# An adaptive attention layer with a mixture-of-experts FFN: the counts and ranks of twelve batches moved ahead of the last batch's mixes

## The chip, the cores and the metric

The program runs on one core of one Trainium2 chip. The core has a matrix engine (TensorE, PE in the rows), VectorE (DVE), ScalarE (ACT), GpSimd (POOL) and SyncE (SP), each with its own queue of instructions; they meet through semaphores only. The metric is the device time of one execution in microseconds; lower is better. All arithmetic is float32, part of it in the form fp32r that splits a value into a high and a low part.

## The reference

Sixteen batches of 128 rows with 128 features go through two layers with one residual:

```
xn   = layernorm(x)
q    = l2norm(xn @ Wq) * q_scale            (16 heads of 64)
k, v = xn @ Wkv, one null key and value in front; k l2-normed
sim  = 8 * q.k + relative-position bias, causal mask
y    = layernorm(softmax(sim) @ v @ Wout) * g_out
out  = x + shared_expert(y) + sum over the two best of 7 experts: w_e * expert_e(y)
expert(h) = (silu(h @ g.T) * (h @ u.T)) @ d.T          (128 -> 352 -> 128)
w: softmax over the router's logits, the two largest, renormalised
```

Of the 2048 rows each goes to two of seven experts, so which rows an expert works on is known only on the chip.

## The kernel before

**Attention.** Every engine runs `step(t)` for t = 0 to 18 (`run_steps`, L280). Step t makes the queries of batch t, the scores of batch t - 1, the turned and mixed probabilities of batch t - 2 (`turn_p`, `mix`), and the projection of batch t - 3. So steps 16, 17 and 18 only drain. In step 17 TensorE also turns the normalised outputs y of batches 0 to 11 (`turn_y`, L1265) and makes their router logits (`logits`, L1274). Step 18 has for TensorE only `mix(3, 3)` and `project()` of batch 15, for ACT `keep_oT(1, 3)`, for VectorE `choose(0)` (L930: the two best experts of each row of batches 0 to 11) and `keep_y()` (L1021: the last projection out of bank 7).

**Routing.** The batches are in two parts, k = 0 (batches 0 to 11) and k = 1 (12 to 15). For a part: `choose(k)` marks the chosen experts; `count(k)` on TensorE (L1282) multiplies these marks by a triangle of ones and by a full matrix of ones, which gives each row's place among the rows of its expert and the totals; `rank(k)` on VectorE (L954) turns that into the row number where the row is to be sent; `weigh(k)` on ACT (L743) and `share_out(k)` on VectorE (L979) make the two shares; `mark(k)` (L949) writes the row's destination beside it. Before the change `count(0)`, `weigh(0)`, `mark(0)`, `rank(0)` and `share_out(0)` stand after step 18; count(0) and rank(0) use bank 6, into which the mixes also write.

**Sends.** GpSimd then issues 32 indirect DMAs (L530), one for each batch and choice: 12 and 12 of part 0, 4 and 4 of part 1. Each writes 128 rows with 128 features, share and destination into a DRAM buffer sorted by expert. The first of a part waits for `row_index_made` and `send_made`. Before send i it also waits until (i - 8) // 2 shared tiles are kept (`down_kept`, at most 13).

**Tiles.** `run_tiles` (L296) runs 16 shared tiles (one a batch, the shared expert) and then 38 routed tiles of 128 rows. A tile goes through four stages, one step each: the high and low parts of its input (yh on ACT L771, yl on VectorE L1118), gate and up matmuls (12 short groups with the down matmuls, L1181), silu and product, turn, down matmuls and the sum (shared: into xs, L1141). Between the first shared tiles stand the routing of part 1 (`between`: `root_y(1)` and `scale_y(3)` after step 0, `turn_y(3)` after 1, `logits(3)` and `choose(1)` after 2, `count(1)` and `rank(1)` after 3, `list_tiles` after 5). The first routed tile needs all 32 sends landed and the list of tiles; SyncE then loads its rows (L381).

L1181 and L1178 are the helpers `mm` and `turn`, so all matmuls and turns have these lines; the tile names tell them apart.

Of the kernel before, what the change touches and what calls it, by code (L numbers as in the profile page):

```python
# [26 lines left out]
def adaln_ffn_kernel(nc: bass.Bass, x, cond, mask, g_norm, wq, wkv, q_scale, k_scale, null_bias, w0, b0, g0,  # L27
# [47 lines left out]
    with ctx:  # L75
# [211 lines left out]

        def logit_bank(b):
            return 5 if b < Y_FIRST else 6

        def turned_bank(t, c):

# [282 lines left out]
        def _(act):  # L575
# [69 lines left out]
            def keep_yT(g):  # L645
                act.wait_ge(y_turned, g + 1)
                nc.scalar.activation(YT[:, g * 512:(g + 1) * 512], bank[y_bank[g]][:, :], ACT.Copy).then_inc(yT_kept, 1)

            def step(t, p, on):
                q = 1 - p  # L650

                def keep_q(c):
                    if on(0):
                        half = slice(c * HALF * P, (c + 1) * HALF * P)
                        act.wait_ge(q_made, 2 * t + c + 1)
                        need(act, scored, NCH * (t - 2) + 2 * c + 2)
                        nc.scalar.activation(qT[:, p, half].rearrange("p (k s) -> p k s", k=HALF),
                                             bank[4][:, :].rearrange("p (k s) -> p k s", k=HALF)[:, :, ::-1], ACT.Copy).then_inc(q_kept, 1)
# [10 lines left out]
                def exp(c, back):  # L669
                    if on(back):  # L670
                        b = t - back
                        act.wait_ge(maxed, NCH * b + c + 1)
                        for h in range(c * HC, (c + 1) * HC):
                            v = Pb[:, b % 2, h, :]
                            last = nc.scalar.activation(v, v, ACT.Exp, bias=low[:, b % 2, h:h + 1],  # L675
                                                        accum_out=den[:, b % 2, h:h + 1])
                        last.then_inc(exped, 1)
# [26 lines left out]

                if t == NB + 1:
                    exp(3, 2)
                keep_q(0)
                keep_pT(0)
                square_q(0)
# [30 lines left out]

            run_steps(act, step)

            def weigh(k):  # L743
                b = slice(PARTS[k].start, PARTS[k].stop)
                act.wait_ge(gap_made, k + 1)
                nc.scalar.activation(share[:, 1, b], share[:, 3, b], ACT.Exp).then_inc(gap_exped, 1)

            act.wait_ge(biasm_first, 2 * NB)
            act.wait_ge(biasm_made, 2 * NB)
            act.wait_ge(y_normed, Y_FIRST // 4)  # L750
            nc.scalar.activation(send[0][1][:, :, 0:D], y_sb[:, 0:Y_FIRST, :], ACT.Copy).then_inc(send_made[0][1], 1)
            weigh(0)

            def step(u, m, lap, kind):
                if kind(3):
# [36 lines left out]
        def _(dve):  # L792
            done = 0

            def own(ins):

                nonlocal done
                done += 1
                ins.then_inc(dve_step, 1)
                dve.wait_ge(dve_step, done)  # L800
# [129 lines left out]
            def choose(k):  # L930
                b, n = slice(PARTS[k].start, PARTS[k].stop), len(PARTS[k])
                dve.wait_ge(logits_made, k + 1)
                lb, eb = L[:, b, :], equal[:, b, :]
                own(nc.vector.tensor_tensor(lb, bank[logit_bank(b.start)][:, 0:NB * NE].rearrange("p (b e) -> p b e", b=NB)[:, b, :],
                                            rbr[:, :].unsqueeze(1).to_broadcast([P, n, NE]), ALU.add))
                for m in range(TOP):

                    own(nc.vector.tensor_reduce(best[:, m, b], lb, AX_X, ALU.max))
                    own(nc.vector.tensor_tensor(eb, lb, spread(best[:, m, b], NE), ALU.is_equal))
                    own(nc.vector.scalar_tensor_tensor(eb, eb, -float(NE),  # L940
                                                       iota7[:, :].unsqueeze(1).to_broadcast([P, n, NE]), ALU.mult, ALU.add))
                    own(nc.vector.tensor_reduce(share[:, 0, b], eb, AX_X, ALU.min))
                    own(nc.vector.tensor_tensor(chosen[:, m, b, :], eb, spread(share[:, 0, b], NE), ALU.is_equal))
                    if m == 0:
                        own(nc.vector.scalar_tensor_tensor(lb, chosen[:, 0, b, :], 2 * NEG, lb, ALU.mult, ALU.add))
                nc.vector.tensor_tensor(load[:, b, :], chosen[:, 0, b, :], chosen[:, 1, b, :], ALU.add).then_inc(load_made, 1)
                nc.vector.tensor_tensor(share[:, 3, b], best[:, 1, b], best[:, 0, b], ALU.subtract).then_inc(gap_made, 1)

            def mark(k):  # L949
                b = slice(PARTS[k].start, PARTS[k].stop)  # L950
                for m in range(TOP):
                    nc.vector.tensor_copy(send[k][m][:, :, DEST_AT].bitcast(I32), dest[:, m, b]).then_inc(send_made[k][m], 1)

            def rank(k):  # L954
                b, n = slice(PARTS[k].start, PARTS[k].stop), len(PARTS[k])
                up, pad = run_up[k], PADS[k]
                dve.wait_ge(sort_consts, 5)
                dve.wait_ge(ranks_made, k + 1)
                tot = bank[6][:, (2 * k + 1) * P:(2 * k + 1) * P + n * NE].rearrange("p (b e) -> p b e", b=n)
                base = eoff[:, :] if k == 0 else run_up[0][:, 0, PADS[0] + Y_FIRST - 1, :]  # L960
                nc.vector.tensor_copy(totals[:, b, :], tot)
                nc.vector.tensor_tensor(up[:, 0, pad, :], tot[:, 0, :], base, ALU.add)
                own(nc.vector.tensor_copy(up[:, 0, pad + 1:pad + n, :], tot[:, 1:n, :]))
                own(nc.vector.tensor_tensor(place[:, b, :], bank[6][:, 2 * k * P:2 * k * P + n * NE].rearrange("p (b e) -> p b e", b=n),
                                            totals[:, b, :], ALU.subtract))
                side, far = 0, 1
                while far < n:
                    own(nc.vector.tensor_tensor(up[:, 1 - side, pad:pad + n, :], up[:, side, pad:pad + n, :],
                                                up[:, side, pad - far:pad - far + n, :], ALU.add))
                    side, far = 1 - side, 2 * far  # L970
                assert side == 0
                own(nc.vector.tensor_tensor(place[:, b, :], place[:, b, :], up[:, side, pad:pad + n, :], ALU.add))
                for m in range(TOP):
                    last = nc.vector.tensor_tensor(placed[:, m, b, :], chosen[:, m, b, :], place[:, b, :], ALU.mult)
                own(last)
                own(nc.vector.tensor_reduce(row_of[:, :, b], placed[:, :, b, :], AX_X, ALU.add))
                nc.vector.tensor_copy(row_index[:, :, b], row_of[:, :, b]).then_inc(row_index_made, 1)
# [9 lines left out]
            def step(t, p, on):  # L987
# [33 lines left out]
                def keep_y():  # L1021
                    if on(3):
                        dve.wait_ge(y_made, t - 2)
                        nc.vector.tensor_copy(y_sb[:, t - 3, :], bank[7][:, 0:D])
                        nc.vector.bn_stats(y_bst[:, t - 3, :], bank[7][:, 0:D]).then_inc(y_kept, 1)
                        if t > 3 and t - 4 != Y_FIRST - 1:
                            gather_y(t - 4)
# [25 lines left out]
                    nc.vector.tensor_scalar(router_wT[:, 0:NE], bank[2][:, 0:NE], gocol[:, 0:1], None, ALU.mult).then_inc(router_kept, 1)  # L1053
                if t == NB + 2:
                    choose(0)
                keep_y()
                if t > 1:
                    invert(0, 1)
# [42 lines left out]
                nc.vector.tensor_scalar(tile_expert[:, RING:RING + ROUTED], tile_float[:, :], 1.0, None, ALU.add)  # L1101
                nc.vector.scalar_tensor_tensor(tile_row[:, :], iota_tile[:, :], float(P), tile_skip[:, :], ALU.mult, ALU.add).then_inc(table_made, 1)

            mark(0)
            rank(0)
            share_out(0)
            own(nc.vector.memset(h_sb[:, :, I:ICH * IC], 0.0))

            def step(u, m, lap, kind):
# [65 lines left out]
        def _(pe):  # L1175
# [4 lines left out]
            def mm(out, a, b, start, stop):  # L1180
                return nc.tensor.matmul(out, a, b, start=start, stop=stop, skip_group_check=True)  # L1181
# [100 lines left out]
            def count(k):  # L1282
                pe.wait_ge(load_made, k + 1)
                pe.wait_ge(sort_consts, 5)
                b, n = slice(PARTS[k].start, PARTS[k].stop), len(PARTS[k])
                load_flat = load[:, b, :].rearrange("p b e -> p (b e)")
                mm(bank[6][:, 2 * k * P:2 * k * P + n * NE], before[:, :], load_flat, True, True)
                mm(bank[6][:, (2 * k + 1) * P:(2 * k + 1) * P + n * NE], ones[:, :], load_flat, True, True).then_inc(ranks_made, 1)

            def step(t, p, on):  # L1290
                q = 1 - p
# [90 lines left out]
                def turn_sums():  # L1382
                    if on(0):
                        pe.wait_ge(sums_kept, t + 1)
                        turn(bank[7][:, P:2 * P], sums_sb[:, :]).then_inc(sums_turned, 1)

                queries(0)
                turn_p(0)
                mix(3, 3)
# [37 lines left out]


            pe.wait_ge(oT_kept, 2 * NB)
            count(0)  # L1430

            expert_regs = [pe.alloc_register(f"expert_reg{k}") for k in range(RING + 2)]

            def load_experts(r):
# [87 lines left out]
```

## Time and profile before

| | |
|---|---|
| median of 3 runs | 437.17 us (432.62 to 437.86) |
| profiled execution | 437.97 us |
| its span | 436.2 us |
| TensorE busy, matmul / weight load | 359.3 us (82%) / 297.6 us (68%) |
| VectorE busy | 291.2 us (67%) |
| ScalarE busy | 279.5 us (64%) |
| GpSimd busy | 228.7 us (52%) |
| mean granted clock of TensorE | 0.923 |

In the span, attention lasts until about 277 us, the shared tiles until about 321, the routed tiles from 328 to about 420, and the last 16 us collect the results. The busy shares are means over these stages; what matters for a change between attention and tiles is the order of a few dozen instructions there, and so the rows come from timelines.

### The profile page before, as it was taken

Reading aid. Unit: us, or ns where it says so; the run is one execution under the profiler, and the core shown is the slowest. Engines: PE = TensorE matmul, PEld = TensorE weight load, DVE = VectorE, ACT = ScalarE, POOL = GpSimd, SP = SyncE. Lnnn points to the kernel's source line nnn. Section 1 sums busy time; section 2 is a strip of 40 time slices with the busy share of each in tenths; the row PEclk is TensorE's granted clock in tenths of the full one; section 3 lists DMA queues with packets and bytes.
Section 4 is the critical chain, followed back from the end, with each engine's and each line's share of the span. In section 5 each row is a group of like instructions: output and inputs, shape, how many; then the busy total and the mean of one; then the engine's idle time right before and its main releaser. Section 6 shows DMA issues by size and latency. Waiting matters only on the chain. (4 is left out here: it accounts for less than half of the span.)

```text
span 436.2 us, 10247 instructions
## 1 busy us (share of the span) xinstructions
PE 359.3 (82%) x2921; PEld 297.6 (68%) x2922; DVE 291.2 (67%) x1144; ACT 279.5 (64%) x935; POOL 228.7 (52%) x253
## 2 busy tenths in 40 slices
PE   0286776999999999999997989587948999999930
PEld 0275655677777777777775647487948999899920
DVE  2838385888888898888889893568524555555514
ACT  1374684999999999999996783345523444444410
POOL 5024833688766667667772542076750444444430
PEclk9997995999999999999999687859997999999995
DMA  6726199970000000000000000011111222121118
GB/s 187 198 78 198 52 221 207 207 141 2 2 2 2 3 2 2 3 0 2 2 2 2 1 2 0 2 50 51 55 43 45 57 61 61 49 60 58 39 19 271
DMA packets 39479, 26.54 MB, mean 61 GB/s; under 512 B 4465, under 2 KB 37131, under 8 KB 39439
## 3 DMA queue, kind: packets, MB, share of 16 engines
q1 hardware_dynamic: 33680, 19.55, 20.1%
q0 software_dynamic: 2240, 4.23, 2.9%
q10 hardware_dynamic: 3518, 2.26, 1.8%
q8 instruction: 20, 0.33, 0.3%
q14 instruction: 21, 0.16, 0.1%
HBM read 12.89 MB, written 13.54 MB: 61 GB/s over the span
## 5 line engine op out<-in xcount | busy, mean ns | idle before, releaser
L675 ACT ACTIVATE p_space<-p_space,low 128x129 f32<-128x129 f32 x256 | 99.0, 392 | 6.3 <-DVE low L1011 6.3
L494 POOL TENSOR_TENSOR p_space<-p_space,inv 128x516 f32<-128x516 f32 x64 | 67.0, 1049 | 66.1 <-DVE inv L1019 66.1
L1007 DVE SCALAR_TENSOR_TENSOR p_space<-bank,rn,biasm_space 128x129 f32<-128x129 f32 x256 | 72.1, 344 | 22.2 <-PE bank L1181 21.9
L485 POOL TENSOR_TENSOR biasm_space<-bias,madd 128x516 f32<-128x516 f32 x64 | 75.6, 1193 | 7.4 <-DVE p_space L1007 7.3
L536 POOL DMA_INDIRECT result_rows<-oT_space,dest_ring x38 | 37.3, 982 | 60.3 <-DVE dest_ring L1147 60.3
L760 ACT ACTIVATE biasm_space<-bank 128x384 f32<-128x384 f32 x54 | 26.6, 492 | 58.3 <-PE bank L1178 58.2
L1178 PE MATMUL bank<-ident,p_space 128*128 128x128 f32 (+1 forms) x272 | 48.5, 297 | 2.4 <-POOL p_space L494 2.1
L675 ACT ACTIVATION_READ_ACCUMULATOR p_space<-p_space,low 128x1 f32 x256 | 48.6, 190 | 0.0
L1181 PE MATMUL bank<-DT,biasm_space 128*128 (+1 forms) x324 | 46.5, 281 | 1.3 <-ACT biasm_space L760 1.3
L1181 PE MATMUL bank<-GH,yh 128*128 (+1 forms) x108 | 41.3, 382 | 6.8 <-DVE yl L1118 6.8
L690 ACT ACTIVATE pT<-bank 128x512 f32<-128x512 f32 x64 | 37.3, 583 | 13.7 <-PE bank L1181 12.5
L1011 DVE TENSOR_REDUCE low<-p_space 128x4 f32<-128x516 f32 x64 | 44.2, 691 | 2.2
L1181 PEld LDWEIGHTS bank<-DT,biasm_space 128*128 128x128 f32 x324 | 43.6, 196 | 2.3 <-issue 1.8
L1181 PE MATMUL bank<-pT,V 128*64 128x256 f32 x256 | 44.6, 433 | 0.1
L1181 PEld LDWEIGHTS bank<-KB,q_space 64*128 64x128 f32 x512 | 33.5, 193 | 15.8 <-issue 9.8
L1181 PE MATMUL bank<-KB,q_space 64*128 64x129 f32 x512 | 42.8, 298 | 1.1 <-DVE p_space L1007 1.1
L1178 PEld LDWEIGHTS bank<-ident,p_space 128*128 128x128 f32 (+1 forms) x272 | 31.3, 147 | 12.6 <-issue 4.6
L1181 PE MATMUL bank<-xnT,wq_sb 128*128 128x128 f32 x256 | 36.3, 286 | 1.6 <-ACT sq L666 1.6
L1178 PE MATMUL bank<-ident,biasm_space 128*128 128x128 f32 x179 | 31.4, 293 | 6.6 <-DVE biasm_space L884 3.9
L1181 PEld LDWEIGHTS bank<-xnT,wq_sb 128*128 128x128 f32 x256 | 31.9, 196 | 7.2 <-issue 5.2
L1181 PE MATMUL bank<-GH,yl 128*128 (+1 forms) x108 | 36.2, 335 | 0.0
L1181 PE MATMUL bank<-GL,yh 128*128 (+1 forms) x108 | 36.2, 335 | 0.0
(217 smaller groups left out, 682.8 us busy)
## 6 DMA issues: line engine op xcount, KB each, us to landing
sent_rows<-fill_row SPq DMA_DIRECT2D x2, 1950.0 KB, 23.0
sent_rows<-fill_row SPq DMA_DIRECT2D x2, 1885.0 KB, 19.1
q_space<-sent_rows SPq DMA_DIRECT2D x38, 65.0 KB
xs<-in_x_dram SPq DMA_DIRECT2D x4, 256.0 KB, 6.4
bias<-bias_rows SPq DMA_DIRECT2D x1, 1024.0 KB, 6.0
xnT<-result_rows ACTq DMA_DIRECT2D x4, 256.0 KB, 6.1
xn<-result_rows SPq DMA_DIRECT2D x4, 256.0 KB, 5.2
out_dram<-xs SPq DMA_DIRECT2D x4, 256.0 KB, 2.4
```

Of the source, the lines that this page charges most:

```text
L485: nc.gpsimd.tensor_tensor(biasm[:, b % 2, heads, :], bias[:, heads, :], madd[:, b:b + 1, :].to_broadcast([P, HC, KEYS]), ALU.add).then_inc ...
L494: nc.gpsimd.tensor_tensor(v, v, spread(inv[:, b % 2, heads], KEYS), ALU.mult).then_inc(p_normed, 1)
L536: nc.gpsimd.indirect_dma_start(out=result_dram[:, :], out_offset=bass.IndirectOffsetOnAxis(ap=dest_ring[:, m:m + 1], axis=0), in_=result[: ...
L675: last = nc.scalar.activation(v, v, ACT.Exp, bias=low[:, b % 2, h:h + 1], accum_out=den[:, b % 2, h:h + 1])
L690: nc.scalar.activation(pT[:, c % 2, :], bank[turned_bank(t, c)][:, :], ACT.Copy).then_inc(p_kept, 1)
L760: nc.scalar.activation(hT[:, (m - 3) % 2, :], bank[4 + (m - 3) % 2][0:IC, 0:ICH * P], ACT.Copy).then_inc(hT_kept, 1)
L1007: last = nc.vector.scalar_tensor_tensor(Pb[:, q, h, :], src, rn[:, q, h:h + 1], biasm[:, q, h, :], ALU.mult, ALU.add)
L1011: nc.vector.tensor_reduce(low[:, q, c * HC:(c + 1) * HC], Pb[:, q, c * HC:(c + 1) * HC, :], AX_X, ALU.max, negate=True).then_inc(maxed, 1)
L1178: return nc.tensor.transpose(out, in_, ident[0:n, 0:n])
L1181: return nc.tensor.matmul(out, a, b, start=start, stop=stop, skip_group_check=True)
```

## The change

It moves the routing of part 0 into step 18. On TensorE `count(0)` now stands at the head of step 18, ahead of `mix(3, 3)` and `project()` of batch 15. On ACT `weigh(0)` stands at the head of that step. On VectorE `mark(0)`, `rank(0)` and `share_out(0)` follow `choose(0)` directly and so come before `keep_y()` of batch 15. As the mixes still use bank 6 then, the counts of part 0 go into bank 3, and TensorE first waits until ACT has copied the turned y out of it; part 1 keeps bank 6. The conditions before the sends are unchanged.

```diff
+        def count_bank(k):
+            return (3, 6)[k]
...
+            def weigh(k):
+                b = slice(PARTS[k].start, PARTS[k].stop)
+                act.wait_ge(gap_made, k + 1)
+                nc.scalar.activation(share[:, 1, b], share[:, 3, b], ACT.Exp).then_inc(gap_exped, 1)
...
+                if t == NB + 2:
+                    weigh(0)
                 keep_q(0)
                 keep_pT(0)
                 square_q(0)
...
-            weigh(0)
...
-                tot = bank[6][:, (2 * k + 1) * P:(2 * k + 1) * P + n * NE].rearrange("p (b e) -> p b e", b=n)
+                tot = bank[count_bank(k)][:, (2 * k + 1) * P:(2 * k + 1) * P + n * NE].rearrange("p (b e) -> p b e", b=n)
...
                 if t == NB + 2:
                     choose(0)
+                    mark(0)
+                    rank(0)
+                    share_out(0)
                 keep_y()
...
-            mark(0)
-            rank(0)
-            share_out(0)
             own(nc.vector.memset(h_sb[:, :, I:ICH * IC], 0.0))
...
-                mm(bank[6][:, 2 * k * P:2 * k * P + n * NE], before[:, :], load_flat, True, True)
-                mm(bank[6][:, (2 * k + 1) * P:(2 * k + 1) * P + n * NE], ones[:, :], load_flat, True, True).then_inc(ranks_made, 1)
+                if k == 0:
+                    pe.wait_ge(yT_kept, y_bank.index(count_bank(0)) + 1)
+                mm(bank[count_bank(k)][:, 2 * k * P:2 * k * P + n * NE], before[:, :], load_flat, True, True)
+                mm(bank[count_bank(k)][:, (2 * k + 1) * P:(2 * k + 1) * P + n * NE], ones[:, :], load_flat, True, True).then_inc(ranks_made, 1)
...
+                if t == NB + 2:
+                    count(0)
                 queries(0)
                 turn_p(0)
                 mix(3, 3)
...
             pe.wait_ge(oT_kept, 2 * NB)
-            count(0)
```

## Rows read from the trace of the kernel before

**Rows 1.** The page: busy tenths and TensorE's granted clock in 40 slices.
```profile
PE   0286776999999999999997989587948999999930
...
PEclk9997995999999999999999687859997999999995
```
**Rows 2.** Chain of waits, in time: start us, length us, what.
```profile
309.63 1.63 PE bank L1181 x12
...
311.60 1.63 PE bank L1181 x12
...
323.30 2.27 DMA sent_rows<-p_space,row_index
...
326.44 1.86 DMA q_space<-sent_rows
...
328.82 3.04 PE bank L1181 x12
```
**Rows 3.** GpSimd's timeline: start us, length us, engine, what, [idle before <-releaser].
```profile
282.54 1.21 POOL L530 DMA_INDIRECT sent_rows<-bias,row_index  x1 [18.28 <-DVE bias L984]
...
296.69 0.96 POOL L530 DMA_INDIRECT sent_rows<-bias,row_index  x1 [0.30 <-issue]
299.16 0.96 POOL L530 DMA_INDIRECT sent_rows<-madd,row_index  x1 [1.51 <-DVE xs L1141]
...
304.29 0.96 POOL L530 DMA_INDIRECT sent_rows<-madd,row_index  x1 [0.38 <-DVE xs L1141]
...
323.30 0.96 POOL L530 DMA_INDIRECT sent_rows<-p_space,row_index  x1 [0.30 <-issue]
```
**Rows 4.** VectorE's timeline, from the choice of part 0 to shared tile 1.
```profile
271.53 0.16 DVE L947 TENSOR_TENSOR share<-best 128x12 f32<-128x12 f32 x1
277.18 0.29 DVE L1024 COPY xn<-bank 128x128 f32<-128x128 f32 x1 [5.49 <-PE bank L1181]
...
277.68 0.14 DVE L952 COPY bias<-dest 128x12 int32<-128x12 int32 x1
...
277.86 0.24 DVE L961 COPY o_space<-bank 128x84 f32<-128x84 f32 x1
...
281.58 0.11 DVE L1107 MEMSET biasm_space<- 128x64 f32 x1
281.73 0.29 DVE L1118 TENSOR_TENSOR yl<-xnT,yh 128x128 fp32r<-128x128 f32 x1
...
285.56 0.28 DVE L1118 TENSOR_TENSOR yl<-xnT,yh 128x128 fp32r<-128x128 f32 x1
...
298.09 0.28 DVE L1141 TENSOR_TENSOR xs<-bank,xs 128x128 f32<-128x128 f32 x1
```
**Rows 5.** TensorE's timeline, attention's last steps to the first routed tile.
```profile
255.30 0.66 PE L1178 MATMUL bank<-ident,p_space 128*128 128x128 f32 x4 [2.05 <-POOL p_space L494]
...
272.03 1.95 PE L1181 MATMUL bank<-pT,V 128*64 128x256 f32 x8
...
277.07 0.68 PE L1181 MATMUL bank<-o_space 128*128 128x84 f32 x4
282.17 0.63 PE L1181 MATMUL bank<-GH,yh 128*128 128x352 f32 x1 [4.42 <-DVE yl L1118]
...
289.01 1.71 PE L1181 MATMUL bank<-router_wT,xnT 128*128 128x7 f32 x8
...
328.35 0.47 PE L1178 MATMUL bank<-ident,q_space 128*128 128x128 f32 x1 [6.93 <-DMA q_space<-sent_rows]
```
**Rows 6.** ScalarE's timeline in step 18 and after.
```profile
274.03 0.60 ACT L702 ACTIVATE oT_space<-bank 128x512 f32<-128x512 f32 x1 [1.36 <-PE bank L1181]
...
276.00 0.50 ACT L771 ACTIVATE yh<-xnT 128x128 fp32r<-128x128 f32 x2
```
**Rows 7.** Busy us (count) by stretch: PE, PEld, DVE, ACT, POOL; clock; DMA; GB/s.
```profile
257.00:258.00 1.00, 1.00 (x5) 0.24 (x4) 0.97 (x5) 1.00 (x6) 1.00 (x2) 0.50 0.00 0
281.00:294.00 13.00, 10.39 (x41) 9.90 (x42) 8.37 (x44) 5.40 (x11) 8.89 (x9) 0.50 0.12 42
```

More of the change, by code:

```diff
@@ L741, in _ @@
             run_steps(act, step)
[L743 to L746, printed above, removed]
             act.wait_ge(biasm_first, 2 * NB)
@@ L963, in rank @@
                 own(nc.vector.tensor_copy(up[:, 0, pad + 1:pad + n, :], tot[:, 1:n, :]))
-                own(nc.vector.tensor_tensor(place[:, b, :], bank[6][:, 2 * k * P:2 * k * P + n * NE].rearrange("p (b e) -> p b e", b=n),
+                own(nc.vector.tensor_tensor(place[:, b, :], bank[count_bank(k)][:, 2 * k * P:2 * k * P + n * NE].rearrange("p (b e) -> p b e", b=n),
                                             totals[:, b, :], ALU.subtract))
```

## The prediction

> **What bounds the kernel now.** I read the page's slices first. They show two holes of TensorE behind the attention steps, one in slice 26 and one in slice 30 of 40 (272 to 283 and 316 to 327 us), with a low granted clock in the slices around the first [rows 1]. Then I read the chain of waits backwards from the first routed tile. The group of matmuls at 328.82 is released by the load of the tile's rows (1.86 us, issued at 326.44), which waited for the landing (2.27 us) of the last of 32 indirect sends that GpSimd issues [rows 2]. TensorE's turn of that tile starts at 328.35 after 6.93 us of idle, so it had run out of shared tiles at 321.4 [rows 5]. So ahead of 328 us the row of sends decides, not the tiles.
>
> What sets the row of sends is in GpSimd's timeline [rows 3]. Sends go out every 1.265 us: (323.30 - 304.29) / 15 = 1.267. The first starts at 282.54 after 18.28 us of idle, released by the shares that VectorE writes. The twelfth starts at 296.69; the thirteenth, which would follow at 297.95, starts at 299.16, because its pace condition wants two shared tiles kept. The seventeenth waits 0.38 us instead of the usual 0.30, so the fourth tile's condition just touches. From 299.16 the last send is 19 sends later: 299.16 + 19 x 1.267 = 323.2, against 323.30. **Hence the time of the second shared tile, not the start of the sends, sets the first routed tile.**
>
> What sets the second shared tile is in VectorE's timeline [rows 4]: its sum into xs is written at 298.09, at the end of an unbroken line of VectorE work that began when the last projection was ready at 277.18. That line is: keep_y 0.50 us (to 277.68), mark(0) 0.18 (to 277.86), rank(0) and share_out(0) 3.72 (to 281.58), the memset 0.15, and then yl of tile 0 at 281.73, root_y(1) and scale_y(3) until yl of tile 1 at 285.56, and so on. TensorE starts tile 0 at 282.17 after 4.42 us of waiting for that yl [rows 5].
>
> **The change, part by part.** The profiled run took 437.97 us for a span of 436.2, 0.8 above the median of 437.17; I work out a difference in its trace and take it off the median.
>
> (a) choose(0) ends with the gap at 271.53 + 0.16 = 271.7 [rows 4]. VectorE then idles for 5.49 us until the last projection. The change puts mark(0), rank(0) and share_out(0) in this hole.
>
> (b) TensorE's count(0), four matmuls and 0.68 us at the full clock [rows 5], moves ahead of mix(3, 3) of batch 15. TensorE runs eight mix matmuls without a gap from 272.03, the last four of which (273.0 on) belong to this step. It reaches the count at 273.0, when VectorE has finished the choice; bank 3 was copied out in step 17, ahead of the logits. So neither of its waits costs anything. But the count is in line before mix, keep_oT and project. Nothing hides it: it delays y_made by its own length. It runs mostly at 1.2 GHz, where eight logits matmuls of the same weight size take 1.71 us, so four take 0.85 [rows 5]. Ends: 0.5 (three quarters of the 0.68, the first of four weight loads under the mix before) to 0.85; I take 0.7, between them. The 0.68 us that it frees after the projection is worth nothing, since TensorE waits there anyway.
>
> (c) ACT's weigh(0) moves ahead of keep_oT(1, 3). ACT is idle for 1.36 us before that copy (274.03), and the gap is made at 271.7, before this hole opens at 272.7 [rows 6]. It is one activation over 128x12, shorter than the 0.25 us of one yh copy, and lies in the hole: cost 0, and 0.25 without it. The two yh copies at 276.00 move by the 0.7 us and stay ahead of VectorE.
>
> (d) VectorE: the count ends at 273.0 + 0.7 = 273.7, rank(0) starts 0.11 later as it does now (277.75 to 277.86), and rank and share_out take 3.72 as now: until 277.5. The delayed projection comes at 277.18 + 0.7 = 277.88. So the whole 3.9 us fits, with 0.35 us to spare; if the count is slower, both move together.
>
> (e) After the projection: keep_y 0.50, memset 0.15, then yl of tile 0 at 277.88 + 0.65 = 278.53 instead of 281.73. **Shift: 3.9 removed (0.18 + 3.72) less 0.7 added = 3.2 us.** All of TensorE, ACT and VectorE from tile 0 on goes by these, so the second shared tile moves by 3.2.
>
> (f) GpSimd: row_index is ready at about 276.8 and the shares at 277.4, so the first send moves from 282.54 to about 278.4, 4.1 us sooner. Send 13 waits for the second tile as before: 299.16 - 3.2 = 295.96. The additional 0.9 us of head start is lost in a longer wait. The last send: 320.1. GpSimd has nothing else queued behind these sends but the results of routed tiles.
>
> (g) The routed tiles start at 328.35 - 3.2 = 325.15, with shared tiles done at 318.2, so the 6.9 us hole stays. From there on no instruction changes: full carry to the end.
>
> Sum: 437.97 - 3.2 = 434.8 for the profiled execution, 437.17 - 3.2 = **434.0** by the median.
>
> **Where a rule weighs against this sum.** The granted clock is 0.50 (1.2 GHz) in 257 to 258 us, soon after an idle of only 2.05 us on TensorE that ended at 255.30; it is also 0.50 in all of 281 to 294, from within the 4.42 us hole on, and full in the slices behind it [rows 1, 5, 7]. After the change the hole is some 1.1 us (277.8 to 279.0), but yl of tile 1 still comes 3.8 us behind that of tile 0 [rows 4], so TensorE idles again behind one tile's matmuls, and small ones follow. I therefore take the clock to stay at its low level for tiles 0 to 2, as now.
> The Trainium skill ("TensorE: Matmul & The Clock Gate", HAM oscillation) says the opposite may hold: it is long idle gaps between bursts of matmuls that bring the clock to its half level, so a kernel that closes them stays warm. By it tiles 0 to 2 would run at full clock; the trace of before does not bear out that short gaps are harmless.
>
> **The rivals.**
> Rival 1, clock stays at 2.4 GHz. Twelve matmuls of a tile take 3.04 us at the low clock and 1.63 at the full one [rows 2]. On the way to the second tile lie half of such a group (0.7 us saved), the logits of 1.71 us, which in the same ratio save 0.8, and turns that save some 0.3: 1.8 in all. The row of sends itself allows it: first send 278.4 plus 12 x 1.267 plus 0.25 for the longer first one is 293.9 for send 13 instead of 299.16, a limit of 5.3 us. Gain 3.2 + 1.8 = 5.0, time 437.2 - 5.0 = 432.2. For it: the longest hole goes. Against it: the 2.05 us idle above.
>
> Rival 2, part of it is given back: VectorE's line meets a count that comes late (TensorE waits at count(0) for choose(0) when its turns and mixes run at full clock, up to 1 us, which mix and projection behind it then pay), or the tiles after the second pace the sends, since the seventeenth has no slack now. Gain 1.5: 435.7.
>
> Rival 3, no gain: the routed start does not hang on tile 2 but on something unmoved. Against it stand the 6.93 us hole and the arithmetic of 19 sends. Time 437.2.
>
> Rival 4, slower, by the pace condition with the clock low for longer. A tile period at the full clock is 311.60 - 309.63 = 1.97 us [rows 2], less than the 2.53 of two sends; at 1.2 GHz it is 1.97 + 1.41 = 3.38, and then every tile paces the row and adds 0.85. Because the fourth tile has no slack, the change turns to a loss from about four additional slow tiles on (4 x 0.85 = 3.4). Six of them (5.1): 437.2 - 3.2 + 5.1 = 439.1. For it: the tiles start sooner while the clock's rise, between 294 and 295 now, need not. Against: from the fourth tile on TensorE is dense, and the clock is full from there [rows 1].
>
> **How the numbers follow.** Chances: forecast 0.63, rival 1 0.13, rival 2 0.11, rival 3 0.05, rival 4 0.08. The forecast's own width: the count's two ends give 433.8 to 434.2, and the three runs shown lie between 432.62 and 437.86, so a median can be 2 us off: 432 to 436. The range takes in most of rival 1 and rivals 2 and 3, and leaves rival 4 out: 430.8 to 437.4. Two per cent, about what a measurement of this kernel can tell from no change, is 8.7 us. No case reaches 428.4 or 445.9; I leave 0.02 and 0.02 for what I don't see: faster 0.02, same 0.96, slower 0.02.
>
> **What would show it.** Right: VectorE has rank(0) ending before 277.9 with the last projection kept at about 277.9; yl of tile 0 near 278.5; TensorE's wait before tile 0 down from 4.4 to about 1 us; first send near 278.4, a wait of 1.5 to 2 us before the thirteenth, last send near 320; the routed tiles' turn near 325.2 after the same hole of 6.9. Wrong: a wait of TensorE at the count, mixes delayed by more than 0.9, a granted clock that is full in 281 to 291 (rival 1), still half after 298 (rival 4), or a routed start that stays at 328.

## The result and the profile after

The changed kernel takes 433.35 us (median of 20 runs, 429.1 to 435.11) against 437.4 (20 runs, 432.62 to 438.29) before. The ratio on record is 0.9936, 95% interval 0.9913 to 0.996: 1.7 to 3.8 us faster, 2.8 in the middle, where the two medians lie 4.05 us apart. It is clear of no change and below two per cent. Forecast were 434.0 and 3.2 us. The executions of one kernel spread here with the mean granted clock: in 35 further runs of the kernel before, those at 0.923 take about 437.3 us and those at 0.938 about 432. The profiled executions (clock 0.923 before, 0.926 after) differ by more than the ratio says, 431.6 against 436.2 us of span, and the first thing to read is how much of that 4.6 is the change.

VectorE's timeline of the changed kernel, from the choice of part 0 to shared tile 1 (columns as in [rows 4]):

```profile
267.31 0.25 DVE L938 TENSOR_TENSOR o_space<-bank,rbr 128x84 f32<-128x84 f32 x1 [2.88 <-PE bank L1185]
...
270.97 0.17 DVE L956 COPY madd<-dest 128x12 int32<-128x12 int32 x1
273.22 0.24 DVE L965 COPY o_space<-bank 128x84 f32<-128x84 f32 x1 [2.08 <-PE bank L1185]
...
276.82 0.17 DVE L989 TENSOR_TENSOR madd<-share 128x12 f32<-128x12 f32 x1
276.90 0.28 DVE L1028 COPY xn<-bank 128x128 f32<-128x128 f32 x1
...
277.58 0.29 DVE L1122 TENSOR_TENSOR yl<-xnT,yh 128x128 fp32r<-128x128 f32 x1
...
293.77 0.28 DVE L1145 TENSOR_TENSOR xs<-bank,xs 128x128 f32<-128x128 f32 x1
```

choose(0) starts at 267.31; before it started at 268.03, so 0.7 us of the difference lies ahead of anything the change touches. From there on: yl of tile 0 comes 10.27 us behind (before: 13.70, so 3.43 sooner), xs of tile 1 another 16.19 (before 298.09 - 281.73 = 16.36). rank(0) starts at 273.22 after 2.08 us of idle, and keep_y follows share_out without any idle.

TensorE and ScalarE of the changed kernel, same stretch:

```profile
271.31 1.12 PE L1185 MATMUL bank<-pT,V 128*64 128x256 f32 x4
272.37 0.74 PE L1185 MATMUL bank<-o_space 128*128 128x84 f32 x4
273.04 0.65 PE L1185 MATMUL bank<-pT,V 128*64 128x256 f32 x4
274.39 2.05 PE L1185 MATMUL bank<-wo_sb,oT_space 128*128 128x128 f32 x16 [0.70 <-ACT oT_space L710]
...
278.02 0.40 PE L1185 MATMUL bank<-GH,yh 128*128 128x352 f32 x1 [1.16 <-DVE yl L1122]
...
323.89 0.47 PE L1182 MATMUL bank<-ident,q_space 128*128 128x128 f32 x1 [6.80 <-DMA q_space<-sent_rows]
```

```profile
271.86 0.19 ACT L655 ACTIVATE share<-share 128x12 f32<-128x12 f32 x1
273.74 0.60 ACT L710 ACTIVATE oT_space<-bank 128x512 f32<-128x512 f32 x1 [1.69 <-PE bank L1185]
```

The count runs without a wait from 272.37 and holds the mixes for 0.67 us, all of it at the full clock (mix(3, 3) behind it takes 0.65 us for four, where eight took 1.95 in [rows 5]); the wait ahead of tile 0 is 1.16 us where it was 4.42 [rows 5]; weigh(0) lies in ScalarE's idle time; the hole before the routed tiles is 6.80 (6.93 before).

GpSimd's timeline of the changed kernel, answering [rows 3], with the first result that a routed tile sends:

```profile
277.90 1.21 POOL L533 DMA_INDIRECT sent_rows<-bias,row_index  x1 [14.63 <-DVE bias L988]
...
292.08 0.97 POOL L533 DMA_INDIRECT sent_rows<-bias,row_index  x1 [0.30 <-issue]
294.83 0.96 POOL L533 DMA_INDIRECT sent_rows<-madd,row_index  x1 [1.77 <-DVE xs L1145]
...
318.95 0.96 POOL L533 DMA_INDIRECT sent_rows<-p_space,row_index  x1 [0.30 <-issue]
334.84 0.99 POOL L539 DMA_INDIRECT result_rows<-oT_space,dest_ring  x1 [14.93 <-DVE dest_ring L1151]
```

The first send is 4.6 us sooner, the thirteenth 4.33 and the last 4.35; 0.72 of each is the earlier choose(0). Send 13 starts 1.06 us behind the start of xs of tile 1, before 299.16 - 298.09 = 1.07.

These marks make a ruler that leaves out what happened ahead of the change. Every length is the difference of two starts in one profile (the first result is at 339.48 in the kernel before); the experiments below are measured with it too:

| us | before | after |
|---|---|---|
| choose(0) to yl of tile 0 | 13.70 | 10.27 |
| yl of tile 0 to xs of tile 1 | 16.36 | 16.19 |
| xs of tile 1 to send 13 | 1.07 | 1.06 |
| send 13 to send 32 | 24.14 | 24.12 |
| send 32 to the first routed turn | 5.05 | 4.94 |
| first routed turn to the first result | 11.13 | 10.95 |
| first to last (38th) result | 81.45 | 81.54 |

From choose(0) to the first result it is 71.45 before and 67.53 after: 3.9 us, of which 3.4 are the first line; that is just above what the times allow (3.8). The granted clock over the stretches, after (columns as in [rows 7]):

```profile
280.00:289.00 9.00, 7.29 (x30) 7.22 (x31) 4.76 (x21) 4.11 (x9) 6.87 (x8) 0.50 0.16 53
290.00:320.00 30.00, 24.77 (x186) 23.92 (x184) 18.07 (x68) 14.55 (x38) 21.62 (x23) 1.00 0.15 50
320.00:327.00 7.00, 3.11 (x13) 3.12 (x14) 0.93 (x4) 0.74 (x2) 0.00 (x0) 0.52 0.25 60
```

It is low under tiles 0 to 2 as forecast, full from 290, and low again from the hole before the routed tiles into the first of them.

### The profile page after: what moved, and what is told of

Its sections match the earlier page's. It is cut to its first block and busy times, and to the rows that moved or that the text cites. A ratio compares the mean times of both kernels' runs of the same rounds, so it can differ in the third digit from the quotient of the medians.

```text
span 431.6 us, 10247 instructions
## 1 busy us (share of the span) xinstructions
PE 357.4 (83%) x2921; PEld 295.8 (69%) x2922; DVE 291.2 (67%) x1144; ACT 279.3 (65%) x935; POOL 228.5 (53%) x253
```

## The experiments

Each experiment ran beside runs of the kernel before, whose medians were 436.91 us (experiments 1, 3 at first, 4 and 5), 436.22 (6 to 9) and 436.51 (2, 3 again, 10 and 11); the ratios are to those. Small effects are read with the ruler, and the times only bound them; a single figure "on the ruler" is the length from choose(0) to the first result. Two things have to be known of it:

- The clock in step 18 is in it. In most profiles it was low there (0.50 from 267 to 272.4 us in the changed kernel), and the first send starts 10.6 to 10.9 us behind choose(0) with the count in its place; in experiments 8 and 9 the clock was full up to the last mixes, and it is 9.1 us, which no edit of theirs explains. So experiments 8 to 11 are also compared from the first send to the first result.
- The time outside the span is not in it. It is 1.72 to 1.85 us in every run of a kernel with the pace condition and 2.06 or more in every run without it (2.06 to 2.18 in experiments 1, 2, 8 and 11, up to 2.86 in 9 and 10). So taking the condition away costs some 0.3 us that no mark shows; the cause stays open.

**1. The changed kernel without the pace condition.**

```diff
-                        need(pool, down_kept, min((TOP * batches.start + n * len(batches) + b - batches.start - 8) // 2, NB - 3))
```

> The changed kernel without the pace condition before the sends (all 32 sends may go as soon as their rows are ready). Theory (the second shared tile paces the row of sends, so the head start of the sends beyond that of the tile is lost): the 1.77 us wait before send 13 vanishes, the last send starts 31 x 1.267 + 0.25 = 39.5 us behind the first, at 277.9 + 39.5 = 317.4 instead of 318.95, and the kernel gains a further 1.5 us: 431.8, about 5.5 below the kernel before, with a hole of 5.3 us of TensorE ahead of the first routed tile. Rival (the pace condition protects the tiles from the sends, or something else releases send 13): shared tiles take longer or send 13 waits all the same, and the time stays at 433.3 or rises.

Measured: 432.89 us, ratio 0.9933 (0.9886 to 0.998). Its GpSimd, TensorE and clock rows:

```profile
277.74 1.21 POOL L532 DMA_INDIRECT sent_rows<-bias,row_index  x1 [14.65 <-DVE bias L987]
...
293.14 0.96 POOL L532 DMA_INDIRECT sent_rows<-madd,row_index  x1 [0.30 <-issue]
...
317.18 0.95 POOL L532 DMA_INDIRECT sent_rows<-p_space,row_index  x1 [0.30 <-issue]
334.03 0.99 POOL L538 DMA_INDIRECT result_rows<-oT_space,dest_ring  x1 [15.89 <-DVE dest_ring L1150]
```

```profile
322.32 0.47 PE L1181 MATMUL bank<-ident,q_space 128*128 128x128 f32 x1 [4.97 <-DMA q_space<-sent_rows]
```

```profile
320.00:327.00 7.00, 4.67 (x19) 4.68 (x20) 1.23 (x5) 1.23 (x4) 0.00 (x0) 0.52 0.20 49
```

The wait before send 13 is gone, last send and routed turn are 1.8 and 1.6 us sooner (1.5 and 1.3 counted from choose(0)), and the shared tiles hardly suffer (16.47 to xs of tile 1, 0.3 more). But the first routed tile now needs 11.71 us to its result, 0.76 more. The reason is in the clock rows: both kernels have 0.52 over 320 to 327, and the one that starts 1.6 us sooner does more of its work in it (19 matmuls against 13). On the ruler 66.98 against 67.53: 0.55 of the 1.3 is left, and the time outside the span takes 0.3 of that. The pace mechanism holds; the expected 1.5 us at the end doesn't.

**2. The kernel before without the pace condition** (the same line).

> The kernel before without the pace condition. Theory (a second shared tile kept at 298.09 sets send 13 at +1.07): the 1.5 us wait there vanishes, the last send starts 39.5 us behind the first (282.54 + 39.5 = 322.0 instead of 323.3), the routed start moves 1.2 us, and some half of that is taken back by the low clock, which lasts as long as before: 0.6 us faster, 436.6. Rival: no change of send 13.

Measured: 436.61 us, ratio 1.001 (0.9971 to 1.0048), which says nothing on 0.6 us. On the ruler 70.60 against 71.45; send 13 starts 0.12 us ahead of xs of tile 1 instead of 1.07 behind, and turn to first result grows to 11.74. Same picture as in 1. Experiments 1 and 2 are also the change once more, on kernels without the condition: the first send moves by 3.77 us (14.46 to 10.69 behind choose(0)) and the first result by 3.6 (70.60 to 66.98).

**3. Only the count and the weighing early**, VectorE's three calls put back behind step 18.

```diff
                     choose(0)
-                    mark(0)
-                    rank(0)
-                    share_out(0)
...
+            mark(0)
+            rank(0)
+            share_out(0)
             own(nc.vector.memset(h_sb[:, :, I:ICH * IC], 0.0))
```

> Only the count and the weighing are early; mark(0), rank(0) and share_out(0) stand behind the last projection, as in the kernel before. Theory (VectorE's 3.9 us of work in its idle hole is the gain, the count ahead of the mixes is a cost of its own 0.7 us): VectorE idles until the projection, yl of tile 0 comes 3.9 us behind the keep_y, and the kernel is 0.4 to 0.7 us slower than the kernel before: 437.9 instead of 437.3. Rival (what counted is TensorE's 0.68 us after the projection, or the clock): a good part of the gain, 1 us or more, stays: 436 or less.

> Once more the kernel with only the count and the weighing early, for a profile in which the low clock does not fall into the projection. Theory: VectorE idles until the projection, about 6 us; yl of tile 0 comes 13.7 + 0.3 us behind the start of choose(0), against 13.7 before and 10.3 in the changed kernel; time 0.3 to 0.7 above the kernel before.

Measured: 436.19 us, ratio 1.0021 (0.9977 to 1.0065), and a second time 436.3, ratio 1.0028 (0.9983 to 1.0073). No gain is seen; 1 us of gain, the rival, lies at or outside the lower ends. The cost of the count alone (0.4 to 0.7 expected) is inside both intervals and so not resolved. Both profiled executions had the clock low from 267 to 297 us, so the expected distance of 14.0 from choose(0) to yl couldn't be read (it was 16.99 there). What can be read is VectorE's own part, in the second profile:

```profile
280.24 0.29 DVE L1028 COPY xn<-bank 128x128 f32<-128x128 f32 x1 [8.84 <-PE bank L1185]
...
284.73 0.29 DVE L1122 TENSOR_TENSOR yl<-xnT,yh 128x128 fp32r<-128x128 f32 x1
```

VectorE is idle up to keep_y again, and yl of tile 0 starts 4.49 us behind keep_y, as in the kernel before (4.55) and not 0.68 as in the changed one.

**4. The pace condition tightened.**

```diff
-... + b - batches.start - 8) // 2, NB - 3))
+... + b - batches.start - 4) // 2, NB - 3))
```

> The changed kernel with the pace condition tightened by two tiles: send i waits for (i - 4) // 2 shared tiles instead of (i - 8) // 2. Theory (a tile's time plus 1.267 us a send sets the last send): send 13 now waits for the fourth tile, which is kept at 299.7, so it starts near 299.95 instead of 294.83, the last one at 299.95 + 19 x 1.267 = 324.0 or a little later, 5.1 us more: 438.4, which is 1 us slower than the kernel before. Rival (the row of sends is set by its start or hidden behind the shared tiles): less than 1 us of difference to the changed kernel, 433 to 434.

Measured: 438.78 us, ratio 1.0066 (1.002 to 1.0112): slower than the kernel before, 5.4 us above the changed one by the medians and 5.7 by the ratios. Its rows:

```profile
278.67 1.21 POOL L533 DMA_INDIRECT sent_rows<-bias,row_index  x1 [14.63 <-DVE bias L988]
...
301.42 0.95 POOL L533 DMA_INDIRECT sent_rows<-madd,row_index  x1 [1.32 <-DVE xs L1145]
...
325.41 0.96 POOL L533 DMA_INDIRECT sent_rows<-p_space,row_index  x1 [0.30 <-issue]
```

From the first send to the thirteenth it is 22.75 us instead of 16.93, from there to the last 23.99. Send 13 starts 1.07 us behind xs of the fourth tile now, which stands 5.56 behind that of the second. Two tiles of delay in a condition cost the whole kernel its two tiles: the release of send 13 sets the start of the routed tiles. The ruler says 74.19, 6.7 more, as the first routed tile met more of a low clock (turn to first result 11.56).

**5. The count behind mix(3, 3)**, in TensorE's 0.70 us wait for oT.

```diff
-                if t == NB + 2:
-                    count(0)
                 queries(0)
...
+                if t == NB + 2:
+                    count(0)
                 project()
```

> The changed kernel with count(0) moved from ahead of mix(3, 3) to behind it and ahead of the projection, where TensorE waits 0.70 us for the copy of oT. Theory (in the profile of the changed kernel rank and share_out end at 276.9, just as the projection is ready, so VectorE has become the bound): the mixes and the projection come 0.65 us sooner, but rank(0) starts 0.65 later (273.9) and keep_y follows at 277.6 instead of 276.9: 0.6 us slower than the changed kernel, 434.0. Rival (the prediction's step: the projection bounds, and the count ahead of it costs its 0.7 us): the kernel gains 0.6: 432.7.

Measured: 433.2 us, ratio 0.9932 (0.989 to 0.9975), not to be told from the changed kernel by time. VectorE and TensorE:

```profile
266.58 0.25 DVE L938 TENSOR_TENSOR o_space<-bank,rbr 128x84 f32<-128x84 f32 x1 [2.85 <-PE bank L1185]
...
272.99 0.25 DVE L965 COPY o_space<-bank 128x84 f32<-128x84 f32 x1 [2.58 <-PE bank L1185]
...
276.68 0.28 DVE L1028 COPY xn<-bank 128x128 f32<-128x128 f32 x1
...
277.36 0.29 DVE L1122 TENSOR_TENSOR yl<-xnT,yh 128x128 fp32r<-128x128 f32 x1
```

```profile
272.21 0.68 PE L1185 MATMUL bank<-o_space 128*128 128x84 f32 x4
272.98 2.05 PE L1185 MATMUL bank<-wo_sb,oT_space 128*128 128x128 f32 x16
274.96 0.48 PE L1185 MATMUL bank<-null_out,pnT 16*128 16x128 f32 x2
277.80 0.40 PE L1185 MATMUL bank<-GH,yh 128*128 128x352 f32 x1 [2.35 <-DVE yl L1122]
```

The projection now ends at 275.4, but VectorE is in rank and share_out until 276.68: yl of tile 0 comes 10.78 us behind choose(0) instead of 10.27. The expected 0.6 is 0.5 there. On the ruler 0.2 is left (67.75), as tiles 0 and 1 met less of a low clock (15.75 us to xs of tile 1 instead of 16.19). So at yl of tile 0 the count ahead of the mixes is the better place: there VectorE's line and the projection end together.

**6. The clock held up over tiles 0 to 2.** One idle matmul of 512 columns behind the projection, two ahead of turn_y(3), into bank 4; nothing reads them.

```diff
+            def warm_up(n):
+                for _ in range(n):
+                    mm(bank[4][:, :], wq_sb[:, 0:P], wq_sb[:, 0:4 * P], True, True)
+            warm_up(1)
             pe.wait_ge(oT_kept, 2 * NB)
...
                 if u == 1:
+                    warm_up(2)
                     turn_y(3)
```

> The changed kernel with idle matmuls into an unused bank: one of 512 columns (0.85 us at the full clock) in TensorE's hole behind the projection and two in the 2.5 us hole ahead of turn_y(3). Their results are not used. Theory (rival 1's mechanism: the low clock of 280 to 289 us, which falls in these holes, delays the second shared tile): the clock stays at 1.00 over tiles 0 to 2, the second tile is kept some 1.5 us sooner, send 13 follows until the row itself binds it (293.3 instead of 294.8), and the kernel gains 1.4 us: 432.0 at the same state of the rest. Rival (the low clock has another cause, the small matmuls of the logits, or the tiles wait on VectorE anyway): clock and send 13 unchanged, 433.3, or 0.5 slower through the matmuls added.

Measured: 432.78 us, ratio 0.9926 (0.9889 to 0.9964). The clock:

```profile
280.00:289.00 9.00, 7.35 (x48) 6.06 (x47) 6.91 (x35) 5.68 (x13) 6.87 (x8) 1.00 0.17 57
290.00:317.00 27.00, 22.51 (x169) 21.66 (x166) 16.45 (x57) 12.44 (x35) 20.60 (x22) 1.00 0.17 55
318.00:327.00 9.00, 4.35 (x18) 4.35 (x19) 1.22 (x5) 0.90 (x3) 0.57 (x1) 0.50 0.20 48
```

The clock is full under tiles 0 to 2, and xs of tile 1 comes 13.94 us behind yl of tile 0 instead of 16.19: 2.25 sooner, where I had put rival 1 at 1.8. Send 13 is then bound by the row itself and starts 15.39 us behind the first (16.93 with the wait). The routed turn comes at 322.65, 1.24 sooner. But TensorE also runs out of shared tiles sooner, the low clock there is as long as 318 to 327, and turn to first result grows from 10.95 to 11.81. The ruler gives 67.15 against 67.53: 0.4 us is left of 2.25, with yl of tile 0 0.3 later behind choose(0) than in the changed kernel.

**7. share_out(0) behind keep_y.**

```diff
                     rank(0)
-                    share_out(0)
                 keep_y()
+                if t == NB + 2:
+                    share_out(0)
```

> The changed kernel with share_out(0) behind keep_y of the last batch instead of ahead of it, so that VectorE's work is the same and the first send starts about 0.4 us later. Theory (the second shared tile sets send 13, the head start of the first sends is slack of 1.5 us): yl of tile 0, send 13 and the end do not move: 433.3, at most 0.2 sooner, as keep_y no longer waits for the 0.6 us of share_out. Rival (the start of the sends counts): 0.4 to 0.6 us slower.

Measured: 433.7 us, ratio 0.9971 (0.9932 to 1.0011). In its profile the first send starts 0.81 us behind yl of tile 0 instead of 0.32, and send 13 again 1.07 behind xs of tile 1 after a wait of 2.09 us: the first send still doesn't set the thirteenth. But the ruler gives 68.36, 0.8 more than the changed kernel. Of that, 0.75 lies between yl of tile 0 and xs of tile 1 (16.94 us), and whether the edit or the clock did it isn't separated. By time it may be up to 0.8% slower than the changed kernel or equal, so the rival of 0.4 to 0.6 us is not excluded. That the wait takes up a later first send is shown, that it costs nothing at the end is not.

**8. Clock held up into the routed tiles**, without the pace condition: five idle matmuls at the head of the step of the first routed tile, into bank 6.

```diff
                     load_experts(-RING)
+                    warm_up(5, 6)
```

> The changed kernel without the pace condition, and with five idle matmuls of 512 columns (4.3 us) into an unused bank in TensorE's hole ahead of the first routed tile, whose results are not used. In the kernel without the pace condition the routed tiles started 1.4 us sooner but at the low clock until 327.0, as long as with it. Theory (that low clock, which begins in the hole, took back 0.7 us of the gain): the clock stays full, the first routed tile takes 1.63 instead of 3.0 us of matmuls and the kernel gains 1.5 to 2 us on the one without the pace condition: 431.0, about 6 below the kernel before. Rival (the routed tiles wait on something else): 432.9, or slower if the idle matmuls delay the first tile.

Measured: 430.33 us, ratio 0.9888 (0.9833 to 0.9944). Its TensorE, GpSimd and clock rows:

```profile
315.51 4.53 PE L1184 MATMUL bank<-wq_sb 128*128 128x512 f32 x10
319.88 0.27 PE L1181 MATMUL bank<-ident,q_space 128*128 128x128 f32 x1
```

```profile
329.29 0.99 POOL L538 DMA_INDIRECT result_rows<-oT_space,dest_ring  x1 [14.32 <-DVE dest_ring L1150]
```

```profile
290.00:400.00 110.00, 104.95 (x764) 99.48 (x763) 62.84 (x271) 51.05 (x145) 50.62 (x52) 1.00 0.19 54
```

The clock is 1.00 from 290 to 400, and turn to first result is 9.41 us, the shortest of all, although the filling ended some 0.8 us too late (5.88 from the last send to the turn, 4.9 to 5.2 elsewhere). Ruler: 63.79, 3.2 less than experiment 1. Half of that is not the filling: 1.6 us are the full clock in step 18 (first send 9.09 behind choose(0), in experiment 1 10.69). From the first send to the first result it is 54.70 against 56.29, 1.6 less: 2.3 from the clock, less 0.7 for the late end. This is where experiment 1's missing gain was.

**9. and 10. Idle matmuls in all holes**, with five and with eight ahead of the routed tiles, no pace condition.

> Both together: no pace condition, idle matmuls in all three holes (one, two and five of 512 columns, results not used). Theory: without the pace condition the sends are bound by their own start (277.9) and 1.267 us a send, so the full clock in tiles 0 to 2 gives nothing more and only that of the routed tiles counts: 431.0, the same as with the idle matmuls ahead of the routed tiles alone, within 0.5. Rival (the clock in tiles 0 to 2 has a worth of its own): a further 1 us or more, 430 or below.

> The kernel with idle matmuls in all holes and no pace condition, with eight instead of five of 512 columns ahead of the first routed tile (6.9 us at the full clock; TensorE had 7.3 us there, and 2.9 of them stayed idle, with a low clock behind them). Theory: the distance from the first routed turn to the first result falls from 12.2 to 9.4 us, as in the kernel that was warm there: 2.8 us less, 428.5. Rival: below 1 us of difference, 430 or more.

Measured: 430.86 us, ratio 0.9894 (0.9837 to 0.995), and 431.62, ratio 0.9894 (0.9835 to 0.9952). With five, the shared tiles ended sooner, 2.93 us of hole were left behind the filling, the clock fell and turn to first result was 12.23 us, the longest; with eight it was 9.53, so 2.7 of the expected 2.8. The rulers are 65.93 and 64.89, but the two met different clocks in step 18 (first send 9.11 and 10.91 behind choose(0)); from there to the first result it is 56.82 and 53.98, the longest and the shortest of the kernels without the pace condition. The times don't follow these 2.8 us; they stand in six runs each, over 4 to 5 us, and in three of the six runs of experiment 10 the time outside the span is 2.7 to 2.9 us, some 0.6 more. So the eight idle matmuls pay in the profile, and not in the times. That the full clock in tiles 0 to 2 gives nothing once the sends aren't paced is borne out: from the first send to the routed turn it is 44.59 and 44.45 us, and 44.58 in experiment 1, where these tiles ran at the low clock.

**11. The count one group of mixes sooner**, without the pace condition and with three idle matmuls ahead of the routed tiles.

```diff
                 turn_pn()
+                if t == NB + 1:
+                    count(0)
                 mix(2, 2)
```

> No pace condition, three idle matmuls of 512 columns ahead of the first routed tile (instead of five, which ended 0.8 us after the rows could be there), and count(0) ahead of mix(2, 2) in step 17, one group of mixes sooner. Theory (without the pace condition the start of the sends sets their end): rank(0) and the first send come 0.6 to 1.1 us sooner, the last send and the routed start too: 0.8 us less than with the count in its place and five idle matmuls, plus up to 0.8 from the shorter filling: 429.2. Rival (TensorE now waits at the count for choose(0), and the projection behind it pays that): the projection and the tiles come up to 1 us later, but the sends do not wait for them, so 430.3 or a little below.

Measured: 429.86 us, ratio 0.9882 (0.983 to 0.9934). The first send starts 9.11 us behind choose(0), as in experiment 8 (9.09). The two came to it in different ways. TensorE in experiment 8, where the count has its usual place:

```profile
265.88 1.08 PE L1184 MATMUL bank<-pT,V 128*64 128x256 f32 x8
...
269.13 0.68 PE L1184 MATMUL bank<-o_space 128*128 128x84 f32 x4 [0.61 <-DVE o_space L949]
```

and here:

```profile
265.87 1.98 PE L1184 MATMUL bank<-pT,V 128*64 128x256 f32 x8
...
268.71 0.68 PE L1184 MATMUL bank<-o_space 128*128 128x84 f32 x4
```

In experiment 8 the mixes ran at the full clock, TensorE came early and waited 0.61 us for the choice. Here the same eight mixes took 1.98 us at the low clock, and the count still starts 3.64 us behind choose(0), at the end of the choice, where the changed kernel with mixes as slow starts it at 5.06. So the earlier place is worth up to 1.4 us when the clock is low there, and, by the wait in experiment 8, nothing when it is full; how much of the 1.4 is the clock's rise at 268.4 isn't separated. Three idle matmuls left 3.19 us of hole, and it is 11.09 us from turn to first result. Ruler 65.05.

Experiments 8 and 11 have the lowest medians, 5.89 and 6.65 us below those of the kernel before that ran beside them; by their ratios it is 1.1 and 1.2%, about 5 us. Their intervals overlap each other and that of the changed kernel (up to 0.9944 and 0.9934, from 0.9913), so that they beat it is likely and not shown by the time alone. From the first send to the first result they are 2.2 and 1.0 us shorter than the changed kernel, and 0.3 of that is lost outside the span.

## Why the prediction was right

**(a), (d), (e): VectorE's hole.** Right. 3.9 us of work fit into it; yl of tile 0 came 3.43 us sooner, forecast 3.2. Experiment 3 shows the other side: without this part no gain. One reading behind (e) was wrong, though: VectorE's work up to the second tile is not an unbroken line. It is busy 8.37 of 13 us in [rows 7] and waits for TensorE, as here in the kernel before:

```profile
290.76 0.19 DVE L934 TENSOR_TENSOR o_space<-bank,rbr 128x28 f32<-128x28 f32 x1 [1.55 <-PE bank L1181]
```

The second tile moved with yl of tile 0 all the same, because TensorE, ACT and VectorE all go by it and the clock there stayed low. Experiment 6 shows what the reading hides: at the full clock that stretch is 2.25 us shorter.

**(b): the count in line ahead of the mixes.** Right in kind: nothing hid its 0.67 us (0.7 said). That the size fits is in part luck: I had taken 0.7 as a value between the clocks, for a count that runs mostly at 1.2 GHz, and it ran at the full clock. The projection was kept only 0.44 later relative to choose(0), as mix(3, 3) ran at the full clock too (0.65 against about 1.0 us). The 0.35 us of room I gave VectorE was not there: keep_y follows share_out with no idle. Experiment 5 shows what that means: VectorE and the projection end together, and VectorE's line 0.5 us later puts yl of tile 0 0.5 later.

**(c):** right, weigh(0) ended at 272.05 in an idle ScalarE.

**(f): head start lost in a longer wait.** Right in kind: 1.06 or 1.07 us from xs of tile 1 to send 13 in every profile where the second tile releases it. Experiments 1, 2 and 4 move the condition and confirm it. The size was off: the first send gained 0.3 us more than send 13 and not 0.9 (counted from choose(0), 3.92 and 3.61), since share_out ended together with the projection and not ahead of it, and the tile gained more than forecast. The wait grew from 1.51 to 1.77 us; the 1.5 to 2 said doesn't follow from the 0.9 either, which would have made it 2.4.

**(g): full carry to the end.** Right here, and for a reason I had not weighed. The hole and the first routed tile both moved with the clock's course (11.13 against 10.95 us from turn to first result). It is no rule: in experiments 1, 2 and 6 the routed start gained 1.2 to 1.5 us more (counted from choose(0)), and 0.6 to 0.9 of it went into the low clock under the first routed tiles. Had I costed those edits by this step, I would have been wrong, and the expectation of experiment 1 was.

**The rivals.** Rival 1's clock did not come: 0.50 from 280 to 289. Its mechanism is real (2.25 us when forced, 1.8 said), but of its further 1.8 us only 0.4 reached the first result when it was forced. The Trainium skill ("TensorE: Matmul & The Clock Gate", HAM oscillation) ties the half clock to long idle gaps between bursts of matmuls. With the gap ahead of tile 0 cut from 4.42 to 1.16 us the clock was still 0.50 under tiles 0 to 2, so the trace doesn't bear out that the long gap alone had lowered it; with matmuls in the gaps (experiments 6, 9 and 10) it was full, which agrees. To the end that paid little until the last gap before the long stage was filled too. Rival 2 needs a wait at the count. In the profiled execution there was none; experiments 8 and 9 show it where the clock was full in step 18, 0.61 us in both, less than the 1.6 by which the first send came sooner there. Rival 3 falls with the routed turn at 323.89. Rival 4 needs a late release, and experiment 4 shows that one costs fully; its own lever, slow tiles that pace the row, wasn't tested, and its trigger was absent: the clock was full from 290.

## What to carry to other kernels

Before costing an earlier start, find the last condition that releases the chain: here a pace condition on the second tile, so that 3.9 us of head start of the sends were worth the 3.6 that this tile gained. A gain ahead of a hole of the matrix engine need not arrive behind it: look at the granted clock on the far side, and price the first work there at both levels. When runs spread by more than the effect, measure between two marks in one profile, one ahead of the change and one where all paths have met, and check what the clock did between them: in experiment 8 it made half of the difference.

## What the runs showed of the hardware

- The same instructions take 9.4 to 12.2 us from the first routed turn to the first result, in step with the granted clock over the 7 us behind the turn: at 1.00 9.41 and 9.53, at 0.75 to 0.78 10.89 to 11.13, at 0.72 to 0.74 11.18 to 11.28, at 0.64 to 0.68 11.56 to 11.81, at 0.57 12.23 (all fourteen profiles).
- Five idle matmuls (ten instructions in the trace, 4.53 us in the row) into an unused bank, in a hole of about 5 us, bought 2.3 us (11.71 to 9.41) and cost 0.8 where they ran past the arrival of the rows. Where 2.9 or 3.2 us of the hole were left behind the filling (experiments 9 and 11) the clock was low again (12.23 and 11.09 us).
- The kernel before was profiled only at a mean granted clock of 0.923. In the profiles of experiments 7, 8, 9 and 11, whose instructions up to choose(0) are those of the changed kernel, the clock is 0.89 to 1.00 over 235 to 250 us instead of 0.77, and choose(0) starts at 265.1 to 265.5 us instead of 266.6 to 268.2. That this is also what parts the runs of the kernel before is likely and not shown.
- The pace condition of the 32 indirect sends protects nothing that the rows show: without it the second shared tile came 0.3 us later in experiment 1 and no later in experiment 2. A row without any sends beside the tiles wasn't run.
